# The cast of the next images moved to the end of the attention, and its low half from GpSimd to VectorE, in a two-image vision transformer layer

## The reference

```python
h = L0_tok_ref(x, W_proj, b_proj)                 # 196 patches of 768 numbers -> 192
h = concatenate([cls_tok, h], axis=1)             # 197 tokens an image
h = h + attn(layernorm(h))     # for e in 4: q, k, v (12 heads of 16), window of 64 keys, softmax, wo;
                               # then silu(fused @ w_gate.T) * (fused @ w_up.T)
h = h + ffn(layernorm(h))      # expert = argmax(softmax(h @ gate_w + gate_b - gate_center));
                               # gelu(h @ w1[expert] + b1) @ w2[expert] + b2
```

## Time and profile before

| | |
|---|---|
| median of 3 runs | 4430.29 us (4427.25 to 4430.92) |
| the profiled execution's own time | 4427.28 us |
| its span in the trace | 4425.5 us |
| busy: PE, DVE, ACT, POOL | 88%, 80%, 68%, 25% of the span |
| granted TensorE clock, mean over the span | 0.975 |
| 32 turns | from about 91 us to about 3978 us |

### The profile page before, as it was taken

One profiled execution on the slowest core, in us unless ns is written; L12 is line 12 of the kernel. 1 busy time (PEld: TensorE's weight loads), 2 busy tenths in 40 slices (PEclk: granted clock), 3 DMA queues, 4 the chain that ended last, 5 costly groups with the idle time before them and its releaser, 6 DMA issues. The chain is left out here.

```text
span 4425.5 us, 120288 instructions
## 1 busy us (share of the span) xinstructions
PE 3916.1 (88%) x41966; PEld 2888.2 (65%) x41966; DVE 3534.6 (80%) x9633; ACT 3025.5 (68%) x9620; POOL 1093.8 (25%) x1496
## 2 busy tenths in 40 slices
PE   3998988998898988988898988989988898987998
PEld 2666666666666666666666666666666666665776
DVE  4888888888888888888888888888888888885665
ACT  2777777767777777777777777777677777773443
POOL 0222222222222222222222222222222222221222
PEclk7999999999999999999999999999999999998999
DMA  5122221111111222211111112222211111115664
GB/s 183 42 51 51 51 51 47 45 47 47 39 36 47 51 51 51 51 47 47 45 47 47 30 46 51 51 51 51 49 46 47 47 48 31 45 48 187 210 215 151
DMA packets 254292, 285.69 MB, mean 65 GB/s; under 512 B 69289, under 2 KB 236755, under 8 KB 244098
## 3 DMA queue, kind: packets, MB, share of 16 engines
q1 hardware_dynamic: 230242, 210.41, 18.7%
q10 hardware_dynamic: 4608, 38.73, 2.8%
q0 software_dynamic: 18912, 29.35, 2.0%
HBM read 123.49 MB, written 39.28 MB: 37 GB/s over the span
## 5 line engine op out<-in xcount | busy, mean ns | idle before, releaser
L867 ACT ACTIVATE p_s<-bank,smin 128x128 f32<-128x128 f32 (+1 forms) x6144 | 1828.3, 377 | 179.8 <-DVE smin L948 161.7
L948 DVE TENSOR_REDUCE smin<-bank 128x3 f32<-128x384 f32 (+1 forms) x2048 | 1135.5, 554 | 218.8 <-PE bank L722 190.5
L742 PE MATMUL bank<-ident_s,p_s 128*128 128x128 f32 (+1 forms) x6144 | 883.9, 253 | 28.9 <-DVE pt_f L953 7.9
L717 PE MATMUL bank<-masks_s,mask_id_s 128*128 128x384 f16 (+1 forms) x2048 | 675.2, 330 | 30.6 <-DVE qt_f L919 16.3
L742 PEld LDWEIGHTS bank<-ident_s,p_s 128*128 128x128 f32 (+1 forms) x6144 | 601.3, 142 | 139.1 <-issue 104.0
L722 PE MATMUL bank<-stacks_f 128*128 128x256 f16 (+3 forms) x4096 | 679.8, 247 | 0.0
L894 POOL TENSOR_TENSOR w_s<-o_raw 128x192 f32<-128x192 f32 (+1 forms) x512 | 307.3, 600 | 1175.0 <-DVE o_raw L941 1175.0
L953 DVE TENSOR_TENSOR pt_f<-bank,pt_f 128x384 f16<-128x384 f32 x1024 | 554.3, 541 | 0.0
L858 ACT CAST pt_f<-bank 128x384 f16<-128x384 f32 x1024 | 512.5, 500 | 0.0
L722 PEld LDWEIGHTS bank<-stacks_f 128*128 128x128 f16 (+1 forms) x4096 | 431.0, 105 | 123.0
L249 PE MATMUL bank<-zt,wqkv_s 128*128 128x394 f16 x1920 | 375.2, 352 | 113.6 <-PEq L1011 61.6
(11 more groups left out here) (132 smaller groups left out, 6470.0 us busy)
## 6 DMA issues: line engine op xcount, KB each, us to landing
stacks_f<-qt_f SPq DMA_DIRECT2D x768, 73.9 KB, 2.1
stacks_f<-kt_f SPq DMA_DIRECT2D x1536, 36.9 KB, 2.1
wx_t<-wx_d SPq DMA_DIRECT2D x36, 1344.0 KB
x_raw<-x_t_dram ACTq DMA_DIRECT2D x32, 1182.0 KB
rec_t<-rec_d SPq DMA_DIRECT2D x36, 582.0 KB, 3.9
stacks_f<-w_dram SPq DMA_DIRECT2D x2, 1536.0 KB
wx_d<-w_s SPq DMA_DIRECT2D x8, 384.0 KB
v_f<-v_f SPq DMA_DIRECT2D x192, 4.1 KB
```

The source lines that it names most:

```text
L717: nc.tensor.matmul(ps, mask_id_s[:, 0:rows], masks_s[:, m0:m0 + HU * kn], start=True, stop=False)
L742: mm = nc.tensor.transpose(turned[:, j * rows:j * rows + rows], p_slot(u)[:, k0:k0 + 128], ident_s[0:rows, 0:rows])
L867: ins = nc.scalar.activation(p_slot(s)[:, j * kn:j * kn + kn], bank[s % SR][0:rows, j * kn:j * kn + kn], ACT.Exp, scale=-1.0, bias=smin[0: ...
L948: nc.vector.tensor_reduce(least, ps, AX_X, ALU.min).then_inc(S["min_ready"], 1)
```

## The change

- The cast of the images leaves ScalarE's projection stage. It stands now in ScalarE's attention program at step 67 (`UNITS + LAG_HI`), behind the cast for the last unit (L858) and ahead of the tail's casts (L876). It waits for the load and for the 72 patch matmuls of this turn, since it writes over the `x_s` that they read.
- GpSimd's subtraction is gone. VectorE does it in six pieces of 394 columns (`image_lows`): piece 0 in the tail behind the low half of the turned output's block (1, 1), pieces 1 to 3 behind that of the last block, pieces 4 and 5 behind the low halves of the next turn's tokens (`low_of`).
- The load of the pair after next is issued by ScalarE as the first thing in the turn, and no longer at the end of its projection stage.
- The semaphore `x_lo` and TensorE's wait for it are gone; the barrier stands between the pieces and the patch matmuls.
- The second pair has to be split ahead of the first turn, so the block before the loop casts it on ScalarE and subtracts it in one instruction on VectorE, behind the memsets that end VectorE's program there.

```diff
--- before.py
+++ after.py
@@ -206,7 +206,7 @@
         names = """patch_mm embedded z1_ready z2_ready z1t_mm z1t_hi z1t_lo z2t_mm z2t_hi z2t_lo var_ready rstd_ready
             proj_mm proj_hi proj_lo v_dup stacked0 stacked1 stacked2 scores_mm min_ready p_ready edge_ready pt_mm pt_hi pt_lo pv_mm
             o_copied o_summed o_rcp_ready o_ready ot_mm ot_hi ot_lo gu_mm sig_ready dve_own h_moved
-            tail_ready lg_mm lg_read onehot_ready pos_mm pos_read pos_ready x_hi x_lo""".split()
+            tail_ready lg_mm lg_read onehot_ready pos_mm pos_read pos_ready x_hi""".split()
         S = {n: sem(n) for n in names}
         nums = sorted(s.num for s in S.values())
         assert nums == list(range(nums[0], nums[0] + len(nums)))
@@ -494,6 +494,9 @@
             @block.scalar
             def _(act):
                 high_of(act, 4, zt1, "z1t_mm", "z1t_hi")
+                act.wait_ge(x_in, 32)
+                act.wait_ge(S["patch_mm"], 4)
+                nc.scalar.copy(x_s[:, 0], x_raw).then_inc(S["x_hi"], 1)
 
             @block.gpsimd
             def _(pool):
@@ -520,6 +523,8 @@
                 dve.wait_ge(wx_out, 16 * (3 * E + 2))
                 nc.vector.memset(pt_late, 0.0)
                 nc.vector.memset(edges, 0.0)
+                dve.wait_ge(S["x_hi"], 1)
+                nc.vector.tensor_tensor(x_s[:, 1], x_raw, x_s[:, 0], ALU.subtract)
 
         nc.all_engine_barrier(sems_to_clear=per_turn)
 
@@ -797,7 +802,6 @@
                             scores(s)
                         for n in patch_at(s):
                             if n == 0:
-                                pe.wait_ge(S["x_lo"], 1)
                                 pe.wait_ge(S["pos_read"], 1)
                             patch_part(pe, n)
                         if 0 <= s - LAG_T < UNITS:
@@ -837,6 +841,7 @@
 
                 @block.scalar
                 def _(act):
+                    act.dma_start(x_raw, x_t[(i + 2) % STEPS]).then_inc(x_in, 16)
                     for n in range(len(proj)):
                         act.wait_ge(S["proj_mm"], n + 1)
                         nc.scalar.activation(proj_target(n, 0), proj_src(n), ACT.Copy,
@@ -844,10 +849,6 @@
                         if n == AT_Z2_OUT:
                             high_of(act, 6, zt2, "z2t_mm", "z2t_hi")
 
-                            act.wait_ge(x_in, 16 * i + 32)
-                            nc.scalar.copy(x_s[:, 0], x_raw).then_inc(S["x_hi"], 1)
-                    act.wait_ge(S["x_lo"], 1)
-                    act.dma_start(x_raw, x_t[(i + 2) % STEPS]).then_inc(x_in, 16)
                     for s in range(PIPE):
                         u = s - LAG_HI
                         if 0 <= u < UNITS:
@@ -868,6 +869,10 @@
                                     p_slot(s)[:, j * kn:j * kn + kn], bank[s % SR][0:rows, j * kn:j * kn + kn],
                                     ACT.Exp, scale=-1.0, bias=smin[0:rows, s % XR, j:j + 1])
                             ins.then_inc(S["p_ready"], 1)
+                        if s == UNITS + LAG_HI:
+                            act.wait_ge(x_in, 16 * i + 48)
+                            act.wait_ge(S["patch_mm"], 4)
+                            nc.scalar.copy(x_s[:, 0], x_raw).then_inc(S["x_hi"], 1)
                         if turned_at(s - OT_HI):
                             e, blk = turned_at(s - OT_HI)
                             for g in range(last_group_of_queries(e) - 2, last_group_of_queries(e) + 1):
@@ -902,8 +907,6 @@
 
 
                     inverse_std(pool, 0)
-                    pool.wait_ge(S["x_hi"], 1)
-                    nc.gpsimd.tensor_tensor(x_s[:, 1], x_raw, x_s[:, 0], ALU.subtract).then_inc(S["x_lo"], 1)
                     nc.gpsimd.tensor_copy(h_in[:, 0:2], h_next[:, 0:2])
                     nc.gpsimd.tensor_copy(h_in[0:ROWS[1], 2:4], h_next[0:ROWS[1], 2:4]).then_inc(S["h_moved"], 1)
                     scatter(pool)
@@ -913,6 +916,11 @@
 
                 @block.vector
                 def _(dve):
+                    def image_lows(k0, k1):
+                        dve.wait_ge(S["x_hi"], 1)
+                        for k in range(k0, k1):
+                            nc.vector.tensor_tensor(x_s[:, 1, k], x_raw[:, k], x_s[:, 0, k], ALU.subtract)
+
                     chain = Chain(dve)
                     for n in range(len(proj)):
                         dve.wait_ge(S["proj_hi"], n + 1)
@@ -991,8 +999,12 @@
                             nc.vector.tensor_tensor(ot[:, 3 * e + blk, 1, :], ot_bank(e, blk)[:, 0:TP],
                                                     ot[:, 3 * e + blk, 0, :], ALU.subtract
                                                     ).then_inc(S["ot_lo"], 1)
-
+                            if (e, blk) == (1, 1):
+                                image_lows(0, 1)
+
+                    image_lows(1, 4)
                     low_of(dve, Z1_BANK, zt1, "z1t_hi", "z1t_lo")
+                    image_lows(4, PKT)
 
                     for tt in range(4):
                         rows = tile_of(tt)[3]
```

## The result

The changed kernel takes **4369.94 us**, median of 4 runs (4367.31 to 4371.85), against 4430.6 us of the kernel before, measured beside it. The ratio is **0.9862**, 95% interval 0.9845 to 0.9879: 1.4% faster, about 61 us. The profiled execution took 4367.31 us. Lines of the changed kernel carry other numbers: the image cast is L875 (before the loop L499), its low half L922 (L527), the high halves L847, the low halves L927, the copies of h_in L910 and L911.

A forecast was written before the change was run, and what follows sets the result against it. TensorE was taken to wait each turn for VectorE's low half of v, delayed by GpSimd's image subtraction and ScalarE's cast. From 4427.3 us, -47.7 + 2.6 + 5.2 - 9.4 = -49.3 gave 4378 us, range 4364 to 4400.

The forecast's parts named there:

- What the change removes: Projection stage: TensorE's wait for VectorE's low half of v goes whole, 1.49 us a turn, -47.7 us.
- ScalarE's cast and the six pieces: Attention's end and tail: 2.17 us cast and VectorE's pieces fit into idle gaps, cost nothing; last gap has 0.1 us left.
- rival 3: Turn's tail: the pieces are not hidden, 3.36 us a turn on the path, 4485 us; chance 0.03.
- The load: Turn's start: 1.18 MB needs some 5 us, its reader comes 80 us later; no cost and no gain seen.
- The prologue: Before the loop: one more VectorE subtraction of 2.60 us opens the loop later, once, +2.6 us.
- The copies of h_in: Turn's start: GpSimd's copies hold VectorE's normalising instructions 0.4 us in 13 turns, +5.2 us; covered in slow-start turns.
- Rival 2: Turn's start: copies of h_in hold normalisation for their whole length, 1.0 us, in every turn; 4405 us, chance 0.10.
- The clock: Attention's end: half of the 13 slow ends at 1.44 us each go, -9.4 us; called a choice, not a reading.
- Rival 5: Whole turn: no slow end and no hold by the copies; 4363 to 4366 us, chance 0.08.
- What would show each step: Trace signs: L355's successor 0.17 us, v wait gone, unslowed turns 119.2 to 119.6 us, 0.1 us idle before the gate.

The follow-up runs named there:

- kernel 1: Kernel before, with one more wait: GpSimd subtracts the images only after VectorE's choice of expert; 4376.8 us, ratio 0.9882.
- kernel 5: Changed kernel with its cast kept, but the subtraction one GpSimd instruction behind the choice of expert, and the load back at the projection stage's end; 4378.8 us, ratio 0.9874.
- Kernel 6: Changed kernel with all six VectorE pieces in one gap, behind the low halves of the next turn's tokens; 4461.2 us, ratio 1.0070.
- kernel 11: Changed kernel with ScalarE's load of the images back at the projection stage's end; 4380.6 us (4369.4 to 4393.3), ratio 0.9874.
- kernel 7: Changed kernel with GpSimd's two copies of h_in held back until the choice of expert is made; 4371.0 us, ratio 0.9862.
- kernel 2: Changed kernel with the images' low half on GpSimd at the turn's start instead of VectorE's pieces, load at the projection stage's end; 4581.9 us, ratio 1.0349.
- kernel 9: Changed kernel plus a VectorE memset of 200 columns (0.225 us) at the end of every turn; 4391.7 us, ratio 0.9908.
- kernel 4: Changed kernel with the images' low half on GpSimd in the tail, after VectorE's four normalising instructions, instead of VectorE's pieces; 4368.9 us, ratio 0.9858.
- kernel 8: Changed kernel plus a VectorE memset of 48 columns (0.098 us) at the end of every turn; 4374.9 us, ratio 0.9867.
- kernels 10: Changed kernel with the h_in copies behind the choice of expert, plus a 200-column memset at the end of every turn; 4384.3 us, ratio 0.9892.
- kernel 12: Changed kernel with ScalarE's load of the images issued in the attention, behind the exponentials of the second unit; 4505.4 us, ratio 1.0184.

## Why the prediction was right, and where it was not

It said 4378 us (4364 to 4400); measured 4369.9, and the mechanism is the one it gave.

- **What the change removes (-47.7).** Right in cause: kernel 1 shows it alone. Sized a little low. Turns without a slow stretch went from 120.66 to 119.10 us where no copy is in the way (kernel 5), 1.56 us against 1.49, some 50 us.
- **ScalarE's cast and the six pieces (0).** Right; nobody waits for either, and the last piece ends against the tanh as close as forecast. The idle time of 0.1 us that was to stand before the gate is not there: the pieces fill it to the end. Kernel 6 shows rival 3's mechanism, pieces that are not hidden, and its price: 1.8 us a turn and the clock's share on top.
- **The load (0, "no gain that I can see").** Right for the changed kernel, wrong as a judgement: with the rest of the change in place, the load at its old place gives TensorE 14 waits, and kernel 11's median is 11 us higher, though its runs spread too far for a verdict on time alone. The prediction looked at how long the load takes, not at what is due while it runs.
- **The prologue (+2.6).** VectorE's added subtraction took 2.56 us and TensorE's first product of the loop came at 93.52 us instead of 91.40: +2.1.
- **The copies of h_in (0.4 us in 13 turns, +5.2).** The hold exists, 0.28 us. But the number of turns was wrong: all 31 behind the first begin slowly, and there it is covered; kernel 7 shows that without it the time is the same. Rival 2 had the hold right and its price wrong: the first two normalising instructions each end 0.11 us behind a copy, as the held one ends behind the subtraction in kernel 2, but they run beside it for most of that time, and both together lose 0.28 us, not the 1.0 of both copies.
- **The clock (-9.4, called a choice).** This term, with the copies', was mis-sized. Slow ends went from 13 to 1, -17.3 us at 1.44 each, and slow starts from 19 to 31, at 0.32 to 0.37 us some +4 to +5. So about -13. The sum was made against a profiled execution, so it is to be held against the profiled one after, 4367.3 us, 11 us below it: 5 from the copies' term that did not come, 3 to 4 from the clock, 2 from the first term and 0.5 from the prologue. The median stands 8 us below. Rival 5's case, no slow end and no hold, is nearly what happened. Half of the slow ends was a choice without a row behind it; that they would fall to one was not foreseen.
- **What would show each step.** L355 at 0.18 us and the wait gone: as given. Turns without a slow stretch, forecast at 119.2 to 119.6 us, did not occur in the changed kernel: its 119.47 holds a slow start. Kernel 5's last 119.10, just under the range. The fast-start turns that were to show the hold did not occur either; kernel 9 has them.

Why three kernels (the change, 4 and 7) settle into one slow start that stands still while kernels 0.1 us a turn longer, or with the work placed otherwise, do not, is not settled. The profiled executions, one of each kernel, show that it is so. Against the sums of the edits it is worth 2 us (kernel 8) to 15 us (kernel 9).

## What to carry to other kernels

Before moving work between engines, look for whom the long GpSimd instruction holds up: here one wait on GpSimd gave 52 of the 61 us, and the same instruction cost 250 us when it stood 0.8 us too early. A large load belongs where no small transfer is due soon; its own length said nothing here. Where the clock changes within a turn, an edit can move the time by more than its sum (13 and 22 us for 7 in kernels 10 and 9), so count slow stretches in both traces before crediting or blaming an edit.

## What the runs showed of the hardware

- A GpSimd instruction that reads SBUF holds a VectorE `tensor_scalar` with one SBUF tensor (L326) and a `tensor_tensor` with two (L355, L383) until 0.03 to 0.12 us behind its own end: up to 5.39 us for a 0.37 us instruction. A `tensor_tensor` of one PSUM and one SBUF operand kept 0.57 us beside it (kernel 4).
- With a memset of 0.098 us at the end of each turn the slow start crept from turn to turn, with a slow end at the end of each round (kernel 8).
- 1.18 MB issued 4.2 us behind the start of six small copies, instead of at the turn's start, cost 135 us over 32 turns (kernel 12): 84 of them are waits of TensorE for a DMA. The rest fits the lower clock behind these waits (0.65 in the row shown) and was not taken apart.
